# A three-layer product network on one core: the first layer's x in one 128-partition transfer per block

## The reference

```
W = W_i.reshape(39, Fk, 128)                       # Fk = 39, then 64, 64
out = relu(einsum('bfd,bgd,fgs->bsd', x, h, W) + bias)   # h = x in layer 0
h, direct = out[:, :64], out[:, 64:]               # layers 0 and 1
direct = out                                       # layer 2
result = concat(direct of the three layers, axis=1).sum(-1)   # [512, 256]
```

## Time and profile before

| | us |
|---|---|
| median of 3 runs (610.09 to 615.98) | 615.74 |
| the profiled execution's own time | 616.65 |
| its span, first to last instruction | 614.9 |
| PE busy | 566.6 (92%) |
| DVE busy | 533.9 (87%) |
| POOL busy | 517.8 (84%) |
| ACT busy | 376.7 (61%) |
| the transfers' packets, as a share of 16 DMA engines | 88.0% |

### The profile page before, as it was taken

One profiled execution on the slowest core, in us unless ns is written; L12 is line 12 of the kernel. 1 busy time (PEld: TensorE's weight loads), 2 busy tenths in 40 slices (PEclk: granted clock), 3 DMA queues, 4 the chain that ended last, 5 costly groups with the idle time before them and its releaser, 6 DMA issues.

```text
span 614.9 us, 8379 instructions
## 1 busy us (share of the span) xinstructions
PE 566.6 (92%) x2032; PEld 386.3 (63%) x2032; DVE 533.9 (87%) x514; ACT 376.7 (61%) x421; POOL 517.8 (84%) x231
## 2 busy tenths in 40 slices
PE   0564679999999999999999999999999999999997
PEld 0332446667676667667676766767666766677665
DVE  2433588889998989999999999999999999999975
ACT  1422375747676675857676675756676675767653
POOL 0344479698998989898998989898989989898995
PEclk9895769999999999999999999999999999999999
DMA  8999999989998999999999999999998999986001
GB/s 205 214 207 212 215 199 228 205 203 191 225 205 210 217 199 215 192 223 196 227 207 221 213 202 226 204 226 181 224 199 212 207 203 225 206 194 150 0 3 34
DMA packets 33073, 118.76 MB, mean 193 GB/s; under 512 B 6817, under 2 KB 6945, under 8 KB 30928
## 3 DMA queue, kind: packets, MB, share of 16 engines
q1 hardware_dynamic: 33056, 118.57, 88.0%
HBM read 118.02 MB, written 0.52 MB: 193 GB/s over the span
## 4 chain that ended last, share of the span: by engine, by line
PE 79%; DMA 7%; issue 5%; POOL 4%; SPq 2%; DVE 1%; ACT 1%; POOLq 0%; ACTq 0%; DVEq 0%
PE acc L470 79%; DMA xwide<-x 5%; POOL z_lo L224 4%; DMA xshift<-x 2%; SPq L251 1%; DVE z_raw L353 1%; ACT z_hi L537 0%; SPq L240 0%; DVE z_whole L353 0%; SPq L234 0%; ACT h L540 0%; ACT last L540 0%; DVE z_lo L224 0%; ACT direct L540 0%; DVE z_hi L222 0%
## 5 line engine op out<-in xcount | busy, mean ns | idle before, releaser
L224 POOL TENSOR_TENSOR z_lo<-z_raw,z_hi 128x1024 fp32r<-128x1024 f32 (+2 forms) x224 | 511.9, 2324 | 82.2 <-ACT z_hi L537 80.2
L537 ACT CAST z_hi<-z_raw 128x1024 fp32r<-128x1024 f32 (+2 forms) x224 | 226.0, 1018 | 159.2 <-DVE z_raw L353 139.1
L353 DVE TENSOR_TENSOR z_raw<-h,xwide 128x1024 f32<-128x1024 f32 x192 | 230.5, 1218 | 26.7 <-ACT h L540 12.8
L470 PE MATMUL acc<-z_hi,w_hi 128*128 128x512 f32 (+2 forms) x560 | 223.4, 468 | 11.1 <-ACT z_hi L537 10.3
L470 PE MATMUL acc<-z_hi,w_lo 128*128 128x512 f32 (+2 forms) x560 | 184.1, 399 | 0.0
L470 PE MATMUL acc<-z_lo,w_hi 128*128 128x512 f32 (+1 forms) x528 | 173.8, 403 | 11.0 <-POOL z_lo L224 5.2
L470 PEld LDWEIGHTS acc<-z_hi,w_hi 128*128 128x128 f32 (+2 forms) x560 | 106.2, 191 | 74.7 <-issue 51.1
L470 PEld LDWEIGHTS acc<-z_lo,w_hi 128*128 128x128 f32 (+1 forms) x528 | 99.1, 190 | 41.0 <-POOL z_lo L224 11.1
L470 PEld LDWEIGHTS acc<-z_hi,w_lo 128*128 128x128 f32 (+2 forms) x560 | 106.4, 190 | 28.8 <-issue 3.8
L470 PE MATMUL acc<-z_whole,w_whole 128*128 128x512 f32 x256 | 121.7, 598 | 0.0
L470 PE MATMUL acc<-z_whole,w 117*128 117x512 f32 x128 | 65.0, 632 | 22.9 <-DVE z_whole L353 22.9
(11 more groups left out here) (16 smaller groups left out, 90.3 us busy)
## 6 DMA issues: line engine op xcount, KB each, us to landing
xwide<-x SPq DMA_DIRECT2D x320, 256.0 KB, 13.8
xshift<-x SPq DMA_DIRECT2D x45, 546.0 KB
xrep<-x SPq DMA_DIRECT2D x48, 78.0 KB
xwide<-w SPq DMA_DIRECT2D x2, 1024.0 KB, 24.8
xshift<-x SPq DMA_DIRECT2D x3, 312.0 KB
xshift<-x SPq DMA_DIRECT2D x3, 234.0 KB
w_whole<-w_rest SPq DMA_DIRECT2D x1, 512.0 KB, 19.5
w<-w0a SPq DMA_DIRECT2D x1, 409.5 KB
```

Of the source, the lines that this page charges most:

```text
L224: return eng.tensor_tensor(lo[0:rows, 0:n, :], z[0:rows, 0:n, :], hi[0:rows, 0:n, :].bitcast(F32), ALU.subtract)
L353: nc.vector.tensor_tensor(dst, in0, in1, ALU.mult).then_inc(made[kind], 1)
L470: return nc.tensor.matmul(dst, w[0:rows, PLACE[layer, t], :], z[0:rows, t - G * g, :], start=first and t == 0, stop=final and t == TILES[l ...
L537: nc.scalar.copy(z_hi[0:rows, slot("PV", pair, par, pos, HI_RING), 0:n, :], src).then_inc(hi_made, 1)
```

## The change

In DRAM, x of layer 0 now stands as an array `x0` of [16 blocks, 128 partitions, 8 slots, 512]: slot 0 is the repeated x, slots 1 to 7 the seven shifted tiles; partitions 117 to 127 hold zeros. In SBUF, `xrep` and `xshift` become one tile, `xfirst` [128, 8, 512], filled by one transfer of 128 rows x 16 KB per block (two for the first block: slots 0 to 4, then 5 to 7). The six semaphore increments become one. ACT's `copy_xrep` now waits for the whole transfer of its block (in the first block, for the first part), and reads slot 0. The transfer is issued where the six were. The DRAM tensor of `xwide` has 40 fields per block in place of 78, its last one a repeat, so that the last group's second transfer reads a run of 4 KB in place of two of 2 KB.

```diff
-        xrep = sb("xrep", [P0, N])
-        xshift = sb("xshift", [P0, T0, N])
+        xfirst = sb("xfirst", [128, 1 + T0, N])
+        xshift = xfirst[0:P0, 1:1 + T0, :]
...
-            def load_rep(j):
-                for a in range(PER):
-                    src = bass.AP(x2.tensor, x2.offset + ROWS2 * N * j, [[N, FIELDS], [1, N]])
-                    sp.dma_start(xrep[a * FIELDS:(a + 1) * FIELDS, :], src).then_inc(xrep_in, 16)
-
-            def load_shift(j, landed, ts=range(T0)):
-                for a in range(PER):
-                    src = bass.AP(x2.tensor, x2.offset + ROWS2 * N * j + N * (T0 * a + ts[0]),
-                                  [[N, FIELDS], [1, len(ts) * N]])
-                    sp.dma_start(xshift[a * FIELDS:(a + 1) * FIELDS, ts[0]:ts[-1] + 1, :], src).then_inc(landed, 16)
+            def load_first(j, landed, slots=range(1 + T0)):
+                src = bass.AP(x0.tensor, x0.offset + 128 * (1 + T0) * N * j + N * slots[0],
+                              [[(1 + T0) * N, 128], [1, len(slots) * N]])
+                sp.dma_start(xfirst[:, slots[0]:slots[-1] + 1, :], src).then_inc(landed, 16)
...
                         sp.wait_ge(*made_all(j, 0))
-                        load_rep(j + 2)
-                        load_shift(j + 2, xshift_in)
+                        load_first(j + 2, xfirst_in)
...
-            load_rep(0)
-            load_shift(0, xshift_first_in, range(0, 2 * G))
-            load_shift(0, xshift_in, range(2 * G, T0))
+            load_first(0, xfirst_head_in, range(0, 1 + 2 * G))
+            load_first(0, xfirst_in, range(1 + 2 * G, 1 + T0))
...
                     if first and g == 0:
-                        dve.wait_ge(xshift_first_in, 16 * PER)
+                        dve.wait_ge(xfirst_head_in, 16)
                     elif g == (2 if first else 0):
-                        dve.wait_ge(xshift_in, 16 * PER * (j + 2))
+                        dve.wait_ge(xfirst_in, 16 * (j + 2))
...
-                act.wait_ge(xrep_in, 16 * PER * (j + 2))
+                if isinstance(j, int) and j == -1:
+                    act.wait_ge(xfirst_head_in, 16)
+                else:
+                    act.wait_ge(xfirst_in, 16 * (j + 2))
                 if not isinstance(j, int) or j >= 0:
                     act.wait_ge(*made_all(j - 1, 0))
-                nc.scalar.copy(xrep_psum[0:P0, :], xrep[:, :]).then_inc(xrep_ready, 1)
+                nc.scalar.copy(xrep_psum[0:P0, :], xfirst[0:P0, 0, :]).then_inc(xrep_ready, 1)
```

More of the change, by code:

```diff
@@ L21 @@
 BB = N // DIM
-ROWS2 = 2 * FIELDS
 SHIFTS = FIELDS // 2 + 1
@@ L123, with cin @@
 assert len(SPLIT0) > 0 and SPLIT_COUNT[1] <= 16 and SPLIT_COUNT[2] <= 16
-def cin(nc, x2, w0a, w0b, w1, w2, w_rest, b, out):
+def cin(nc, x, x0, w0a, w0b, w1, w2, w_rest, b, out):
     with ExitStack() as ctx:
@@ L171, in cin @@
         bias_in = sem("bias_in")
-        xrep_in = sem("xrep_in")
-        xshift_in = sem("xshift_in")
-        xshift_first_in = sem("xshift_first_in")
+        xfirst_in = sem("xfirst_in")
+        xfirst_head_in = sem("xfirst_head_in")
         xw_in = [[sem(f"xw_in{p}_{g}") for g in range(G12)] for p in range(2)]
@@ L244, in load_wide @@
                     first = T12 * e + G * g
[L245 to L250, removed]
+                    src = bass.AP(x.tensor, x.offset + 2 * T12 * N * j + N * first, [[0, HALF], [1, G * N]])
                     sp.dma_start(xwide[HALF * e:HALF * (e + 1), half, G * g:G * (g + 1), :],
@@ L279, in _ @@
             sp.wait_ge(*made_all(-1, 0))
-            load_rep(1)
-            load_shift(1, xshift_in)
+            load_first(1, xfirst_in)
             sp.dma_start(stage[2][:, 0:SPLIT_COUNT[2], :], w2).then_inc(w_staged[2], 16)
@@ L288, in _ @@
             sp.wait_ge(*made_all(0, 0))
-            load_rep(2)
-            load_shift(2, xshift_in)
+            load_first(2, xfirst_in)
             sp.wait_ge(w1_lo_made, 1)
@@ L664 @@
     w2 = tiled(np.asarray(L0_rec_W2))
+    x0 = np.zeros((BLOCKS, 128, 1 + T0, N), np.float32)
+    for a in range(PER):
+        x0[:, FIELDS * a:FIELDS * (a + 1), 0] = x
+        for t in range(T0):
+            x0[:, FIELDS * a:FIELDS * (a + 1), 1 + t] = x[:, (f + T0 * a + t) % FIELDS]
     arrays = {
-        "x2": np.concatenate([x, x], axis=1),
+        "x": np.concatenate([x, x[:, T12 - 1:T12]], axis=1),
+        "x0": x0,
         "w0a": w0a.reshape(P0, T0, SIZE),
```

## The result

The changed kernel took 597.34 us (median of 4 runs, 595.77 to 598.9) against 615.26 us for the kernel before (4 runs). The ratio of the mean times is 0.973, with a 95% interval of 0.967 to 0.979: 2.7% faster, where 1.0% was forecast. Its profiled execution took 597.35 us, 19.3 us less than the 616.65 of the one before, with a span of 595.5 us. The profiled execution of the kernel before was one of its slower ones (its runs reach from 609.9 to 617.45 us in this and the later comparisons), so the 19.3 us that the two traces are apart are some 2 us more than the gain of 2.7%.

The account below looks back on a forecast made before the run. The transfer queue was taken to bound the first 60 us, PE the full stretch later. From 616.65 us, minus 7.3 for x of blocks 0 and 1, plus 0.5 for ACT's wait, came 609.8; range 602.5 to 617.

Parts of the forecast that it names:

- The two regimes: Transfer queue paces the first 60 us or so; PE is full from 165 to 590 us, where shorter transfers gain nothing.
- The price of x: Blocks 0 and 1: x takes 7.9 us at 265 GB/s, against 10.5 and 12.6, gaining 7.3 us.
- The row of 265: Window 17 to 19.5 us, with layer 1's split weights queued: 265 GB/s, taken as the new x's rate.
- awaited by nobody: Three engines without x ran ahead in the queue; giving them x too changes nothing on the landing.
- The port rule: Transfer speed follows SBUF ports reached, 435 GB/s in total: x in 4.8 us, time 603 us; supports the larger gain, 0.14.
- hardly idled there: Block 3: DVE's 3.79 us wait for x goes, worth at most 0.5 us, set to nothing.
- The larger-gain rival: In the start, x at 289 GB/s gains 8.5 us and PE's full clock some 4: 604 us; chance 0.14.
- The signs: Expected in the profile: first product about 12 us, x of block 1 about 44, the next `xwide` product about 51.
- The added wait: Block 2: ACT's copy waits for all of x, 1.9 us at 265 GB/s; cost put at 0.5 us.
- ACT as the bound at block 2: If x gains nothing, ACT stands 6.6 us at its copy and PE idles, costing 5: 622.7 us; chance 0.09.
- The cover of three subtractions: Block 2: three already cast POOL subtractions, 3 x 2.3 us, keep work going while ACT waits.
- The rate of a DMA engine stays as it is: Per-engine rate of x unchanged, so 11% less time, 2.6 us over two blocks: 613 to 616 us; chance 0.22.

Follow-up runs that it names:

- fast_start_only: Changed kernel with x of blocks 0 to 2 in three 128-row transfers each, later blocks in three of 39 rows: 598.04 us, ratio 0.977 to the kernel before.
- slow_start_only: Changed kernel with x of blocks 0 to 2 in three 39-row transfers each, later blocks in three of 128 rows: 618.55 us, ratio 1.010 to the kernel before.
- x_two64: Changed kernel with each block's x as two transfers of 64 rows, partitions 0 to 63 and 64 to 127: 609.26 us, ratio 0.994 to the kernel before.
- x_three39: Changed kernel with each block's x fetched from the new layout as three transfers of 39 rows: 618.86 us, ratio 1.010 to the kernel before.

## Why the prediction was wrong in size

**What bounds the kernel: right.** The two regimes and the worth of nothing beyond the start are shown by the pair of fast_start_only and slow_start_only.

**The price of x: the step that failed.** The sum took "265, the row of the same shape seen where least else is mixed in", 7.9 us for a block's x, and as fastest end 289. Measured: 426 GB/s where only x is under way. x of block 0 ends at about 11.6 (issued at about 2.1, 9.5 us to landing) after w0b at 6.18, in 5.4 us against 10.5; x of block 1 takes 36.18 - 30.91 = 5.3 us with ACT's copy, against 12.6. The two gains are 5.1 + 7.3 = 12.4 us where 7.3 were forecast. The row of 265 was a mixture: of its 118 packets 48 were 4 KB pieces of `xwide` and 57 rows of the split weights, and these 57 took 0.48 us each, against 0.33 in the changed kernel, where all 128 rows of the weights move together. So the row gave neither the rate of one shape alone nor that shape's rate with the engines in step, and I took it for both. I also put the three engines that held no x at nothing, as "awaited by nobody". That they ran ahead is shown by the 24 and 104 rows above; what it cost is not shown by itself.

**The port rule: set aside, and near the mark for x.** The page "SBUF — State Buffer" of the Trainium skill, section "Door 1: The DMA port swizzle", gave, as an estimate, 4.8 us for a block's x and 603 us in sum; I gave that side 0.14, because no row showed more than 289 GB/s. No row could: no transfer of the kernel before was both alone and on all partitions. Where only x was under way it came to 426 GB/s, near that page's 435, and the two 64-row kernels behave as the rule has it, 208 against 415 GB/s. The rule is not enough: 112 rows, on all but 16 partitions, moved at 233. Nor does it reach the measured time, because 603 us has no term for what follows below. And the support that I drew from the trace was false: that `xwide` at 222 GB/s is "near half of 435, which agrees". With 128 rows it stayed nearly as slow, 269 GB/s against 247, and 415 came only with distinct source rows. Two limits gave nearly the same number.

**What else came out larger.** 2.4 us between the end of x of block 0 and 38.99 (8.1 - 0.6 - 5.1), with the same transfers in the queue as before; 1.3 us between 51.58 and 57.89, where layer 2's split weights stand; 1.2 us at block 3, which I set to nothing because PE "hardly idled there"; 1.2 us from 57.89 to the h of the seventh slice; 0.6 us before w0b, which is scatter (w0b lands between 5.6 and 7.2 us in kernels with the same transfers ahead of it). That engines in step carry the following transfers faster too could explain the first two. For the 1.3 us the other traces bear it out: from the first product of block 1 to the next `xwide` product it is 5.55 to 6.3 us with x in 39 or 117 rows, and 4.7 to 5.5 with 128, 64 or 112 (where `xwide` is left as it was), x_two64 with its slow x among them (46.71 to 52.02). For the 2.4 us they do not: that stretch takes 21.7 us in the kernel before and 19.3 in the changed one, but 19.2 in x_three39 (19.45 to 38.68), whose x is in 39 rows too. Its cause stays open. The larger-gain rival also had PE keep its full clock, worth 4 us; the 1.2 us from 57.89 on are all that can be of that.

**The signs.** DVE's first product starts at 10.34 us (about 12 was said), that of block 1 at 36.18 (44), the `xwide` product behind it at 41.23 (51). All three lie the way that was forecast and go further.

**The added wait: right in mechanism.** I expected 1.9 us of ACT at 265 GB/s and a cost of 0.5 us, measured were 1.83 us and none. The two cancel errors: x is faster than assumed, and so is everything ahead of it. The rival, ACT as the bound at block 2, is real: with slow x ACT stood 7.50 us, as against 6.6 worked out. It put the cost of 6.6 us at 5; the series above has some 3 us for 6.84. The cover of three subtractions, 6.9 us, was too large for that case: 3.8 were covered.

**"The rate of a DMA engine stays as it is": wrong.** A 14 KB packet of x of block 1 took 1.17 us before (12 GB/s for its engine), a 16 KB packet 0.71 after (23 GB/s).

## What to carry to other kernels

In these runs x was fast in 128 rows and in 64 rows on every second partition, and slow in 39, in 64 neighbouring ones, in 112 and in 117. So pad an operand like x to 128 rows, and if the rows are repeats, give each a DRAM run of its own. A queue that paces only the start of a kernel is worth its full length there and nothing later, so cost a change of transfers against the stage where somebody waits. Before taking a rate from a window, check that the window holds only that kind of transfer, and when a rate matches a rule's number, find a row that the rule's rival could not give.

## What the runs showed of the hardware

- 64 rows of 16 KB, same bytes and same number of transfers: 208 GB/s on partitions 0 to 63 and 64 to 127, 415 GB/s on even and odd ones.
- 128 rows of 16 KB reached 426 GB/s from DRAM beside running compute, 128 distinct rows of 4 KB 414 to 415. 112 rows of 16 KB moved at 233 GB/s at block 1.
- With x in 39 or 117 rows, 24 of the 128 rows of the weights behind it in the queue moved 9 to 19 us ahead of the other 104: three engines had no x. With 128, 64 or 112 rows all 128 moved together.
- 128 rows of which eight or sixteen read the same DRAM run moved at 229 to 269 GB/s, at 4 and at 8 KB, with neighbouring rows or every eighth one on the same run. That they also lay close together in DRAM was not tried apart.
- A load that DVE needs later and ACT sooner costs by its place in ACT's queue: 7.50 us of waiting cost some 3.5 us, up to 3.2 us cost nothing.
